# Where the first lap's q tiles of an attention layer are computed: five of them between the expert layer's end and the first lap, or three inside the expert layer's last steps and nine in the lap's slots

## The reference, cut to what matters

```python
x = x + tanh(g_ffn[0])   * L0_ffn(layernorm(x), ...)      # the expert layer in front of the seam
x = x + tanh(g_xattn[1]) * L1_xattn(layernorm(x), ctx_512, ...)

# in L1_xattn, 16 heads:
q_big  = einsum('bshk,hkq->bshq', hidden_q @ Wq.T, w_kc_q)   # 192 wide per head
q_big  = q_big * cos + rotate_half(q_big) * sin
q_r    = einsum('bshq,hqr->bhsr', q_big, W_qr)               # 64 wide per head
scores = einsum('bhsr,bhlr->bhsl', q_r, k_r)
attn   = softmax(scores)
ctx    = (attn @ kv_r) @ w_kc_kv.T ;  out = ctx @ Wo.T
```

## Time and profile before

| | |
|---|---|
| median of 3 runs | 552.07 us (551.7 to 552.79) |
| the profiled execution | 549.6 us |
| its span | 547.7 us, 8990 instructions |
| mean granted TensorE clock | 0.961 |
| last steps of the expert layer | about 187 to 207.5 us |
| between the layer and the first lap | about 207.5 to 229.4 us |
| first lap | about 229.4 to 255 us |
| further laps | until about 440 us |

### The profile page before, as it was taken

How to read it: one execution, slowest core, us unless ns; L and a number is a source line. 1 busy time by engine, 2 the same in 40 slices (tenths; PEclk the granted TensorE clock), 3 DMA queues, 4 the chain that set the end, 5 groups by cost and what they waited for, 6 DMA issues and landing times.

```text
span 547.7 us, 8990 instructions
## 1 busy us (share of the span) xinstructions
PE 501.3 (92%) x2727; PEld 383.5 (70%) x2727; DVE 414.7 (76%) x1060; ACT 305.4 (56%) x789; POOL 246.3 (45%) x255
## 2 busy tenths in 40 slices
PE   6886999998998997799999999999999969899986
PEld 3664678876876885467777777777776757678864
DVE  5998599988477759888888888888888874644322
ACT  3744554433635542277777777776668773155541
POOL 0042446765434842465646464554442007445560
PEclk9969799999999999879999999999999996999998
DMA  7659313222421219853717180807003702334426
GB/s 252 210 186 310 120 54 91 87 59 62 145 85 57 89 36 243 162 125 79 157 46 170 35 171 31 186 16 165 1 0 129 345 1 93 101 116 114 128 61 230
DMA packets 40280, 65.02 MB, mean 119 GB/s; under 512 B 4323, under 2 KB 30637, under 8 KB 39984
## 3 DMA queue, kind: packets, MB, share of 16 engines
q1 hardware_dynamic: 37984, 60.31, 39.2%
q0 software_dynamic: 2256, 4.21, 2.4%
HBM read 38.48 MB, written 27.99 MB: 121 GB/s over the span
## 4 chain that ended last, share of the span: by engine, by line
PE 36%; DVE 36%; ACT 12%; issue 9%; DMA 5%; POOL 1%; SPq 1%; DVEq 0%; POOLq 0%; ACTq 0%
PE bank L798 9%; DVE qr L2035 5%; DVE negm L2049 4%; ACT silu L1772 4%; PE bank L1002 4%; PE bank L833 4%; DVE x L2070 3%; DVE qr L2031 3%; ACT qs L1765 3%; DVE qs L2043 2%; DMA moe_x<-xn_slots 2%; PE bank L1018 2%; DVE xn L355 2%; DVE hid L754 2%; DVE silu L752 2%
## 5 line engine op out<-in xcount | busy, mean ns | idle before, releaser
L1407 POOL TENSOR_TENSOR qr<-qr 128x512 f32<-128x512 f32 x48 | 61.7, 1286 | 16.0 <-DVE qr L2035 16.0
L2035 DVE TENSOR_TENSOR qr<-bank,sinq 64x512 f32<-64x512 f32 x96 | 66.1, 689 | 2.2
L1412 POOL TENSOR_TENSOR hid<-silu,rden 128x256 f32<-128x256 f32 x55 | 33.7, 613 | 74.0 <-DVE rden L2054 73.5
L1772 ACT ACTIVATE silu<-bank,negm 128x256 f32<-128x256 f32 x128 | 59.1, 469 | 11.9 <-DVE negm L2049 11.9
L715 POOL TENSOR_TENSOR ffn_w_l<-ffn_raw,ffn_w_h 128x512 fp32r<-128x512 f32 x30 | 39.4, 1313 | 35.6 <-ACT ffn_w_h L727 35.4
L1779 ACT ACTIVATE hid<-silu,rden 128x256 f32<-128x256 f32 x55 | 27.9, 507 | 41.8 <-DVE rden L2054 41.8
L739 ACT ACTIVATE hid_h<-hid 128x512 fp32r<-128x512 f32 x28 | 17.7, 631 | 55.5 <-DVE hid L754 49.2
L2049 DVE TENSOR_REDUCE negm<-bank 128x2 f32<-128x512 f32 x64 | 44.1, 690 | 4.4 <-PE bank L1585 3.1
L957 POOL DMA_INDIRECT y_rows<-moe_y,route_rows x31 | 30.1, 971 | 31.5 <-issue 16.1
L1584 PE MATMUL bank<-ks_h,qs 128*128 128x256 f32 x128 | 40.6, 340 | 2.7 <-ACT silu L1772 1.5
L798 PE MATMUL bank<-xT_h,ffn_w_h 128*128 128x512 f32 x120 | 40.8, 422 | 0.8 <-DVE xT_l L412 0.8
(11 more groups left out here) (245 smaller groups left out, 1327.2 us busy)
## 6 DMA issues: line engine op xcount, KB each, us to landing
xn_slots<-blank SPq DMA_DIRECT2D x8, 2056.0 KB, 12.4
ffn_raw<-in_w_ffn SPq DMA_DIRECT2D x30, 256.0 KB, 2.7
pair_w<-in_pair_w SPq DMA_DIRECT2D x8, 768.0 KB, 5.4
moe_w<-in_w_moe SPq DMA_DIRECT2D x1, 6144.0 KB, 17.9
moe_x<-xn_slots SPq DMA_DIRECT2D x31, 128.5 KB, 2.1
ffn_raw<-in_w_ffn SPq DMA_DIRECT2D x30, 128.0 KB, 2.3
folds<-att_w_raw SPq DMA_DIRECT2D x6, 640.0 KB, 6.4
att_w_raw<-folds SPq DMA_DIRECT2D x6, 384.0 KB, 11.8
```

The source lines that it names most:

```text
L1407: nc.gpsimd.tensor_tensor(qr[n][:, 0, :], qr[n][:, 0, :], qr[n][:, 1, :], ALU.add).then_inc(s_turned, 1)
L1772: last = nc.scalar.activation(ex[u % 2][:, h, :], bank[4 + u % 2][:, h * S:(h + 1) * S], ACT.Exp, bias=negm[:, u % 2, h:h + 1], accum_out= ...
L2035: last = nc.vector.tensor_tensor(by_sin[other, :, :], q2[hs, :, :], sinq[hs, j:j + 1, :].broadcast_to([C, 2, S]), ALU.mult)
```

## The change

Three q tiles of pair 0, (0,0), (0,1) and (0,2), are computed in `mid` of c = 24, 25 and 26; DVE does their cos/sin in the hooks of c = 25 and 26 and in `before_sum`. Behind the layer PE does (1,0), (1,1), the rope product of (0, c = 0), (1,2), the second half's turning and (0,3), and the first lap begins. Tiles (0,4) and (0,5) are computed in its slot 0, (1,3), (1,4) and (1,5) in its slots 4, 5 and 6. Nine cos/sin tiles lie in its slots: (0,3) in slot 0, (0,4) and (0,5) in slot 1, then (1,0) to (1,5) in slots 2 to 7. On ACT, `q_high` of the first half moves ahead of `n_att[1].act_high`. On POOL, `turned` of the first three tiles stands ahead of the last layer's low parts, the others in the lap; slot 7 also does its own tile. Banks of the first tiles change. No DMA, no load and none of the places of `high_part` and `low_part` is changed.

```diff
+        def q_order(i, n):
+            early = ((0, 0), (0, 1), (0, 2), (1, 0), (1, 1), (1, 2), (0, 3), (0, 4), (0, 5))
+            return early.index((i, n)) + 1 if isinstance(i, int) and (i, n) in early else i * 6 + (n + 1)
...
-        Q_AT, FIRST_Q_AT = {0: 1, 1: 2, 3: 3, 4: 4, 5: 5}, {1: 2, 3: 3, 4: 4, 5: 5}
-        COS_AT, FIRST_COS_AT = {0: 0, 1: 1, 2: 2, 4: 3, 5: 4, 6: 5}, {0: 0, 1: 1, 2: 2, 4: 3, 5: 4, 6: 5}
+        Q_AT, COS_AT = {0: 1, 1: 2, 3: 3, 4: 4, 5: 5}, {0: 0, 1: 1, 2: 2, 4: 3, 5: 4, 6: 5}
+        FIRST_Q_AT = {0: ((0, 4), (0, 5)), 4: ((1, 3),), 5: ((1, 4),), 6: ((1, 5),)}
+        FIRST_COS_AT = {0: ((0, 3),), 1: ((0, 4), (0, 5)), 2: ((1, 0),), 3: ((1, 1),), 4: ((1, 2),), 5: ((1, 3),),
+                        6: ((1, 4),), 7: ((1, 5),)}
...
-        FIRST_BANKS = {(0, 0): 6, (0, 1): 2, (0, 2): 0, (0, 3): 7, (0, 4): 6, (0, 5): 7, (1, 0): 3, (1, 1): 1, (1, 2): 0}
+        FIRST_BANKS = {(0, 0): 6, (0, 1): 7, (0, 2): 6, (0, 3): 6, (0, 4): 7, (0, 5): 2, (1, 0): 3, (1, 1): 1, (1, 2): 0}
...
-                turned(0, 0)
-                turned(0, 1)
+                for n in range(JT):
+                    turned(0, n)
                 for st in (ffn1_first, ffn1_second):
                     ffn1.low_gateup(pool, st)
-                for n in range(2, 2 * JT):
-                    turned(0, n)
...
-                    elif (i, n) == (0, 5):
-                        pe.wait_ge(s_cs, 8)
+                    elif (i, n) == (0, 2):
+                        pe.wait_ge(s_cs, 2)
...
+                    if isinstance(i, int) and (i, c) == (0, 1):
+                        pe.wait_ge(s_cs, 2 * 2 * JT)
...
-                              N0 + 2: lambda: comb_pe(route[0][1], pe), 2 * N0 - 2: first_q_step},
+                              N0 + 2: lambda: comb_pe(route[0][1], pe), **{2 * N0 - 4 + n: partial(first_q_step, n) for n in range(JT)}},
...
-                for i, n in ((0, 1), (0, 2), (1, 0), (1, 1)):
-                    q_step(i, i, n)
+                q_step(1, 1, 0)
+                q_step(1, 1, 1)
+                rope_step(0, 0, 1, 0)
+                q_step(1, 1, 2)
                 n_att[1].pe_transpose(pe)
                 n_att[1].pe_whole(pe)
                 q_step(0, 0, 3)
-                q_step(0, 0, 4)
-                rope_step(0, 0, 1, 0)
-                q_step(0, 0, 5)
-                pe.wait_ge(s_cs, 10)
...
                 n_att[1].act_root(act)
+                q_high(0, 0, 0)
                 n_att[1].act_high(act)
                 split_first_tile()
-                q_high(0, 0, 0)
...
-                                    2 * N0 - 5: lambda: n_att[0].low(dve)}, topk_round, first_cos_sin)
+                                    2 * N0 - 5: lambda: n_att[0].low(dve), 2 * N0 - 3: lambda: first_cos_sin(0),
+                                    2 * N0 - 2: lambda: first_cos_sin(1)}, topk_round, lambda: first_cos_sin(2))
...
                 n_att[1].scale(dve, seq)
-                cos_sin(0, 1)
                 n_att[1].low(dve)
-                cos_sin(0, 2)
-                cos_sin(0, 3)
-                cos_sin(0, 4)
                 q_low(0, 0, 0)
-                cos_sin(0, 5)
```

More of the change, by code:

```diff
@@ L8 @@
 from contextlib import ExitStack
+from functools import partial
 import numpy as np
@@ L1234, in shared, with tiles, q_tiles, cos_tiles @@
                 return self.q
[L1236 to L1240, removed]
+            def tiles(self, n, first, at):
+                if self.first:
+                    return [(i, i, tile) for i, tile in first.get(n, ())]
+                return [(self.i, self.b, at[n])] if self.q and n in at else []
+            def q_tiles(self, n):
+                return self.tiles(n, FIRST_Q_AT, Q_AT)
+            def cos_tiles(self, n):
+                return self.tiles(n, FIRST_COS_AT, COS_AT)
             def rope(self, n):
@@ L1418, in slot @@
                         normalise(before[0], before[2])
-                    tile = lap.cos_tile(n - 1)
-                    if tile is not None:
-                        turned(lap.i, tile)
+                    for i, _, tile in lap.cos_tiles(n - 1):
+                        turned(i, tile)
                     m = lap.weights(n)
@@ L1424, in slot @@
                         low_part(lap.i + 1, 1 - lap.b, m)
+                    if n == NU - 1:
+                        for i, _, tile in lap.cos_tiles(n):
+                            turned(i, tile)
                 pool.wait_ge(ffn0.hl, 1)
@@ L1633, in slot @@
                         values(*half)
-                    m = lap.q_tile(n)
-                    if m is not None:
-                        q_step(lap.i, lap.b, m)
+                    for tile in lap.q_tiles(n):
+                        q_step(*tile)
                     if n == NEXT_Q_AT and lap.more:
@@ L1640, in slot, with first_q_step @@
                         project(*batch)
-                def first_q_step():
-                    n_att[0].pe_whole(pe)
-                    q_step(0, 0, 0)
+                def first_q_step(n):
+                    if n == 0:
+                        n_att[0].pe_whole(pe)
+                    q_step(0, 0, n)
                 ffn0.prog_pe(pe, {1: lambda: rows_pe(route[0][0], pe),
@@ L2019, in second_rows, with first_cos_sin @@
                     dve.wait_ge(route[0][1].rowc, 2)
-                def first_cos_sin():
-                    dve.wait_ge(s_trig, 32)
-                    cos_sin(0, 0)
+                def first_cos_sin(n):
+                    if n == 0:
+                        dve.wait_ge(s_trig, 32)
+                    cos_sin(0, n)
                 def cos_sin(i, n):
@@ L2026, in cos_sin @@
                         dve.wait_ge(s_rp, i * (2 * JT) + JT * (n // JT) - JT)
-                    dve.wait_ge(s_q, i * 6 + (n + 1 + 2 * (n >= JT and isinstance(i, int) and i == 0)))
+                    dve.wait_ge(s_q, q_order(i, n))
                     q2 = bank[bank_of(i, n)][:].rearrange("p (b s) -> p b s", b=2)
@@ L2076, in slot @@
                     unit, before = lap.unit(n, 0), lap.unit(n, 1)
-                    half, m, done = lap.q_low(n), lap.cos_tile(n), lap.batches(n, ADDED)
+                    half, done = lap.q_low(n), lap.batches(n, ADDED)
                     heads = () if lap.shared() else (0, 1)
@@ L2099, in slot @@
                         normalise(before[0], before[2], heads)
-                    if m is not None:
-                        cos_sin(lap.i, m)
+                    for i, _, tile in lap.cos_tiles(n):
+                        cos_sin(i, tile)
                 for r in range(AHEAD):
```

## The result

| | median | profiled execution, its span |
|---|---|---|
| before | 552.43 us (551.7 to 552.84, 4 runs) | 549.6, 547.7 |
| changed | 560.14 us (558.8 to 561.2, 4 runs) | 560.52, 558.6 |

The medians differ by 7.7 us. The ratio is 1.0147 (95% interval 1.0118 to 1.0176), that is 8.1 us, and 6.5 to 9.7 by its interval. Forecast was 558.4, 6.3 slower, with 554.5 to 562.0 as the range: inside the range, and at the low edge of what was measured.

What follows compares the result with a forecast made beforehand. PE was taken to bound the layer's last steps, DVE the laps; after the change the fold loads' landing at 235.0 decides. 249.95 + 10.04 + 1.40 = 261.4 against 255.14, so 552.07 + 6.3 = 558.4 us, range 554.5 to 562.0.

Steps and rivals of the forecast that it cites:

- The tiles in the layer's steps, 2.80: Expert layer's last steps: two q tiles cost PE 1.40 each, ending the last gate/up 2.80 later; DVE's share is free.
- The x sum at 211.3: Behind the layer: DVE's adding of the layer's sum to x moves 2.80 later, from 208.49 to 211.3.
- First maximum at 221.65, exps of slot 1 by 226.7: Start of the first lap: first maximum 7.8 us earlier than 229.41; ACT finishes slot 1's exps by 226.7.
- The landing at 235.0: Pair 2's second fold load, behind two slot clears on SP's queue, lands at 235.0 instead of 232.2.
- ACT idle some 8 us (8.3 in the working): Slot 1: ACT reaches the high part of pair 2's weights at 226.7 and waits 8.3 us for the fold loads.
- POOL's adds until 239.85, rope tail 1.73, q_low at 242.8: Queue behind the landing: POOL's adds to 239.85, rope product tail 1.73 at half clock, q copies to 242.8, then q_low.
- Mark at 261.4: First maximum of lap 2: slot 4 at 249.95 plus 10.04 of PE work plus 1.40 gives 261.4, against 255.14.
- rival C: PE stays at half clock, not back at full by slot 5: +9.3 us, 561.4; chance 0.10 together with D.
- The sum, +6.3: Whole kernel: the end moves by what the mark moves, 6.3 us later, 558.4; forecast's chance 0.73.
- Rival A: The landing gates nothing: with loads by 226.7, POOL's queue is the next gate, mark 254.8, -0.3, 551.7; chance 0.10.
- Rival B: DVE is the only bound: it runs through from 221.65, mark 251.5, -3.6, 548.5; chance 0.07.
- The transfer rule of the Trainium skill: Clears and fold loads: about 2.0 us plus bytes at 436 GB/s puts 5.5 MB down at 222, before ACT asks.

Runs made afterwards that it cites:

- experiment 1: Changed kernel with pair 2's two fold loads issued ahead of SP's two slot clears: 553.02 us against 551.62 before, ratio 1.0025.
- 2: Changed kernel with the high and low parts of pair 2's weights moved from slots 1 and 4 to 3 and 5, DMAs unmoved: 552.01 us, ratio 1.0012.
- 4: Kernel before with a third 2056 KB write between the two clears and the fold loads: 558.17 us against 551.62, ratio 1.0116.
- the second time: Changed kernel unedited, run and profiled again in another job: 556.05 us against 548.62 before, ratio 1.0136.
- the last kernel: Changed kernel with fold loads first, POOL's adds of (0,4), (0,5) ahead of unit 1's normalise, dummy PE matmuls (filler) in slots 1 to 4: 545.25 us, ratio 0.9942.
- with POOL's order: Changed kernel with fold loads ahead of the clears and POOL's adds of (0,4), (0,5) ahead of unit 1's normalise: 547.25 us against 548.62, ratio 0.9984.
- the first job: Runs beside 551.62: changed, fold loads first (1.0025); changed, weights' parts in slots 3, 5 (1.0012); before, fold loads first (0.9991); before, third clear (1.0116).

## Why the prediction was right

- **The tiles in the layer's steps, 2.80.** Right to 0.2: PE takes 1.40 a tile without a gap, and DVE's part is hidden.
- **The x sum at 211.3.** It came at 211.80: 0.2 from the gate/up, and 0.3 from L764, DVE's hidden low part, which took 0.99 us where before it took 0.69. The tile behind it started late by as much.
- **First maximum at 221.65, exps of slot 1 by 226.7.** 223.32 and 228.67 in the first profile, 222.00 and 226.8 in the second. In the first, PE's clock was 0.81 in 218 to 222 and 0.76 in 222 to 226, which I had not put in; it cost nothing there, as ACT waited afterwards anyway.
- **The landing at 235.0.** 222.70 + 11.29 = 233.99, a microsecond early. Both durations of landing were as before (18.3 and 11.3), but SP got through the clears in 4.63 us for 5.20 and through the issue of L1343 in 7.91 for 8.59.
- **ACT idle some 8 us (8.3 in the working).** 5.33 in the first profile, 6.94 in the second, as ACT came later and the landing earlier than I had them. That the wait ends at the landing, and what is queued behind it, was as forecast; experiments 1, 2 and 4 show it from three sides.
- **POOL's adds until 239.85, rope tail 1.73, q_low at 242.8.** Adds until 238.6, then 237.44 + 1.97 + 1.72 = 241.13, q_low at 242.39. I had counted four matmuls behind the last add; at half clock the second head's two, which wait for the add of (0,4), outlast the add of (0,5). The landing and the adds were early and this product late, so q_low came within 0.4 of the forecast by misses that partly cancel.
- **Mark at 261.4.** 262.44 and 260.68. In the first profile tile (1,3) took 2.93 at half clock and held up slot 5 by 0.74; I had left that to rival C.
- **The sum, +6.3.** +7.7, and +7.4 the second time. The marks give 7.3 and 5.5 against the one profile of before. I had the end move by what the mark moves; in the first profile it moved by 3.6 more, behind the laps, where single executions differ (below). For the second there is no profile of before from the same job, and where its other 2 us lie is open. The mechanism was right as forecast; that the sum came out as near as 1.4 (1.8 by the ratio) is in part luck.

Rival A named the next gate rightly, POOL's queue, and its condition (loads by 226.7) was made true in experiment 1: 1.4 above before where A had -0.3. Rival B, DVE alone, was reached in no run, but the last kernel, with the gates ahead of DVE taken away one by one, comes near its price: 3.2 under before for 3.6, its mark at 252.29 for 251.5.

The transfer rule of the Trainium skill (DMA: Bandwidth & Descriptors, Anatomy of one DMA) gave, as the estimate in the prediction, a landing at 222. The trace does not agree: 233.99. The Trainium skill gives the rule there for transfers issued from GpSimd. These were issued from SP, behind two clears of 2056 KB; which of the two makes the difference no run here shows.

## What to carry to other kernels

Before work is pulled earlier, look at what each engine meets next in its queue, and when its operands land: an instruction that had 1.8 us to spare before is 5 to 7 us early after, and everything behind it on two in-order engines waits with it. A wait that costs nothing today is tied to the schedule around it; the same reorder of DMAs was worth nothing in the kernel before and some 6 us in the changed one. Once it is gone, go on down the path (queue order, then PE's clock): here the loads first took away most of a loss of 7 us, with POOL's order the kernel could not be told from before (0.9984), and with filler as well it was 2 to 3 us under. And look at where PE's clock falls next: filler in two slots kept it up there and let it fall in the two behind.

## What the runs showed of the hardware

- A small load behind large writes in one queue pays for them: 128 KB landed 11.3 us after issue behind two 2056 KB clears (and its 384 KB neighbour after 18.3), and after 5.5 and 4.6 us when issued ahead of them. A third clear moved the landing by 9.5 us.
- Half 2's rope product takes 1.97 + 1.72 us in the chain of the changed kernel, from 237.44, after PE was idle and short of work, with the granted clock at 0.50 (1.2 GHz) in 234 to 238 and 0.63 in 238 to 242. With filler ahead of it, at 1.00 (2.4 GHz), each of its two parts takes 1.08 in PE's timeline of the last kernel.
- The rope product's matmuls for one head, when they run by themselves, take as long as those for both heads together: 1.97 for two records behind the add of (0,4), and 1.97 for four in the timeline of before (clock 0.50); at 1.00, 1.07 for two in the kernel with loads first and filler, and 1.08 for four in the last one. Operands that come one after the other cost PE the second head's time in full.
- Behind the laps, POOL writes rows to memory by index in sixteen scatters (L951). The gap between the starts of the eighth and the ninth is 1.3 to 1.8 us in eight of the thirteen profiles and 3.2 to 4.0 in five, in kernels of either kind. The five are the first profile of the changed kernel and all four of the first job (551.62 beside them); so it does not go with the change, and whether it goes with the chip, the job or the single execution is open. In these five DVE waits there for something the trace can't name:

```profile
465.71 4.71 another core or an unknown queue
```

It is in the first profile of the changed kernel and not in the one of before, whose spans differ by 10.9 us: 7.3 up to the mark, and of the 3.6 behind it 2.2 are this gap. What it is stays open.
